# The row numbers of a block's store: from VectorE to GpSimd, and a ring of six

## The reference

```
x = x + tanh(g_xattn[0]) * xattn0(layernorm(x), ctx)      # 16 heads, 120 context rows per batch
x = x + tanh(g_ffn[0])   * ffn0(layernorm(x))             # 8 experts, top 2, silu(x Wg) * (x Wu), then Wd; hidden 688
x = x + tanh(g_xattn[1]) * xattn1(layernorm(x), ctx)
x = x + tanh(g_ffn[1])   * ffn1(layernorm(x))             # 8 experts, top 2, relu(x W1)^2, then W2; hidden 256
```

## Time and profile before

| | |
|---|---|
| median of 3 runs | 711.34 us (710.27 to 711.49) |
| span of the profiled execution | 741.8 us |
| PE busy | 659.3 us (89%) |
| DVE busy | 407.1 us (55%) |
| ACT busy | 271.6 us (37%) |
| POOL busy | 221.4 us (30%) |

### The profile page before, as it was taken

How to read it: one execution, slowest core, us unless ns; L and a number is a source line. 1 busy time by engine, 2 the same in 40 slices (tenths; PEclk the granted TensorE clock), 3 DMA queues, 4 the chain that set the end, 5 groups by cost and what they waited for, 6 DMA issues and landing times.

```text
span 741.8 us, 17801 instructions
## 1 busy us (share of the span) xinstructions
PE 659.3 (89%) x6008; PEld 481.6 (65%) x6008; DVE 407.1 (55%) x1375; ACT 271.6 (37%) x531; POOL 221.4 (30%) x405
## 2 busy tenths in 40 slices
PE   8889887789999999999999999989888888789960
PEld 6657666557777777777775555667666656578730
DVE  3888778774444323332332223688888775554416
ACT  4555555542211111121111112467666432244430
POOL 5123434433231111111111111124655344544430
PEclk9999999999999999999999999999999999899995
DMA  9243434552124111101311100601111132443329
GB/s 231 68 136 124 142 123 169 183 178 67 44 101 120 38 36 29 36 30 36 82 33 41 30 15 18 232 30 31 59 60 59 59 101 86 144 122 115 108 72 339
DMA packets 49960, 69.14 MB, mean 93 GB/s; under 512 B 7751, under 2 KB 37319, under 8 KB 49875
## 3 DMA queue, kind: packets, MB, share of 16 engines
q1 hardware_dynamic: 40620, 49.00, 21.8%
q0 software_dynamic: 6528, 17.90, 6.8%
q10 hardware_dynamic: 2727, 1.11, 0.6%
HBM read 45.76 MB, written 22.23 MB: 92 GB/s over the span
## 4 chain that ended last, share of the span: by engine, by line
PE 70%; DVE 14%; issue 5%; another core or an unknown queue 5%; DMA 2%; ACT 2%; POOL 1%; SPq 0%; ACTq 0%; DVEq 0%; POOLq 0%
PE ps L1764 26%; PE ps L1810 16%; DVE m_rows L981 4%; PE ps L1550 4%; PE ps L1787 3%; PE ps L1488 3%; PE ps L1542 3%; PE ps L1505 2%; PE ps L1588 2%; PE ps L1564 2%; DVE x_sb L965 2%; DVE ctx_q L998 1%; PE ps L1516 1%; DVE share L1003 1%
## 5 line engine op out<-in xcount | busy, mean ns | idle before, releaser
L1764 PE MATMUL ps<-w_all,share 128*128 (+1 forms) x720 | 213.2, 443 | 8.2 <-DVE share L1125 5.8
L1764 PEld LDWEIGHTS ps<-w_all,share 128*128 128x128 f32 (+1 forms) x720 | 125.2, 180 | 73.6 <-issue 13.9
L629 POOL DMA_INDIRECT ys_dram<-share,dest_i x72 | 69.1, 960 | 297.1 <-DVE share L1346 247.5
L1810 PE MATMUL ps<-w_all,share 112*128 (+3 forms) x576 | 139.1, 385 | 5.0 <-ACT share L864 4.3
L1810 PEld LDWEIGHTS ps<-w_all,share 112*128 112x128 f32 (+3 forms) x576 | 98.2, 180 | 24.8 <-issue 8.6
L1405 DVE TENSOR_TENSOR share<-share,ps 128x344 f32<-128x344 f32 x72 | 37.0, 514 | 122.1 <-PE ps L1764 54.1
L981 DVE TENSOR_REDUCE m_rows<-ps 128x8 f32<-128x960 f32 x64 | 70.6, 1143 | 14.4 <-PE ps L1505 9.9
L845 ACT COPY share<-ps 128x512 f32<-128x512 f32 x36 | 21.1, 585 | 141.2 <-PE ps L1787 141.2
L600 POOL DMA_INDIRECT xs_dram<-xn,slot_now x64 | 63.6, 994 | 30.0 <-issue 14.0
L840 ACT ACTIVATE share<-ps 128x344 f32<-128x344 f32 x72 | 32.9, 457 | 96.8 <-PE ps L1764 71.4
L577 POOL TENSOR_SCALAR nm<-mv 128x1 f32<-128x1 f32 (+1 forms) x48 | 11.6, 242 | 157.5 <-DVE mv L1021 120.4
(11 more groups left out here) (235 smaller groups left out, 1102.8 us busy)
## 6 DMA issues: line engine op xcount, KB each, us to landing
w_all<-ys_dram SPq DMA_DIRECT2D x16, 512.0 KB, 7.3
share<-xs_dram SPq DMA_DIRECT2D x56, 129.0 KB
w_all<-gate SPq DMA_DIRECT2D x8, 688.0 KB
w_all<-up SPq DMA_DIRECT2D x8, 688.0 KB
w_all<-down SPq DMA_DIRECT2D x8, 560.0 KB
w_all<-w SPq DMA_DIRECT2D x16, 256.0 KB
share<-xs_dram SPq DMA_DIRECT2D x32, 64.5 KB
out<-x_sb SPq DMA_DIRECT2D x8, 256.0 KB, 5.6
```

The costliest lines, as they stand in the source:

```text
L629: g.indirect_dma_start(ys_dram, bass.IndirectOffsetOnAxis(ap=dest_i[:, u:u + 1], axis=0), y_sb[:, u, :], None).then_inc(D_y[u], 16)
L1764: i = t.matmul(ps[0:r, bank, 0:w], xgT[:, k, 0:r], w_all[:, bass.ds(off + (k * UPW[l] + col - EW[l]), w)], start=(k == 0), stop=(k == KT - 1))
L1810: i = t.matmul(ps[0:n, 6, 0:D], h[:, 0:n], w_all[0:r, bass.ds(off + (KT * UPW[l] + c * D - EW[l]), D)], start=(c == 0), stop=(c == KD[l] - 1))
```

## The change

GpSimd computes the row numbers itself, in `store_block`, just ahead of the DMA that uses them; VectorE's `block_rows` is gone with all its calls. The instruction is a tensor_scalar with `spare` as a scalar per partition, where it was a tensor_tensor. GpSimd now has the waits for `xid` and for the store of three blocks before (`D_y`), and one for its own result. `xid` is a ring of six columns in place of three, so that `x_evac(j)` waits for the row numbers of the block six before, made by GpSimd, and no more for those of the block three before. In layer 0 `y_evac` on VectorE still needs the `D_y` wait for `y_sb`, and now has it behind the wait for TensorE. ScalarE's `y_evac` of layer 1 is as it was.

```diff
-        xid = sb("xid", [P, U3])
+        xid = sb("xid", [P, 2 * U3])
...
             def store_block(l, j):
-                u = j % U3
-                g.wait_ge(d_dest, J0[l] + j + 1)
-                g.wait_ge(e_y, J0[l] + j + 1)
+                J, u, w = J0[l] + j, j % U3, (J0[l] + j) % (2 * U3)
+                g.wait_ge(d_xid, J + 1)
+                need(g, D_y[u], 16 * uses(l, j))
+                g.tensor_scalar(dest_i[:, u:u + 1], xid[:, w:w + 1], spare[:, j:j + 1], None, ALU.min).then_inc(g_dest, 1)
+                g.wait_ge(g_dest, J + 1)
+                g.wait_ge(e_y, J + 1)
                 g.indirect_dma_start(ys_dram, bass.IndirectOffsetOnAxis(ap=dest_i[:, u:u + 1], axis=0),
...
                 def x_evac(j):
...
-                    need(v, d_dest, J - U3 + 1)
-                    v.scalar_tensor_tensor(out=xid[:, u:u + 1], in0=xg[:, u, D + 1:D + 2], scalar=be[:, j:j + 1],
+                    need(v, g_dest, J - 2 * U3 + 1)
+                    v.scalar_tensor_tensor(out=xid[:, w:w + 1], in0=xg[:, u, D + 1:D + 2], scalar=be[:, j:j + 1],
...
-                def block_rows(j):
-                    J, u = J0[l] + j, j % U3
-                    v.wait_ge(d_xid, J + 1)
-                    need(v, D_y[u], 16 * uses(l, j))
-                    v.tensor_tensor(dest_i[:, u:u + 1], xid[:, u:u + 1], spare[:, j:j + 1], ALU.min).then_inc(d_dest, 1)
-
                 def y_evac(j):
-                    block_rows(j)
                     v.wait_ge(b_y, j + 1)
+                    need(v, D_y[j % U3], 16 * uses(0, j))
...
                 def blk1(j, u, first, last):
-                    if j >= 2:
-                        block_rows(j - 2)
...
-                    if last:
-                        block_rows(j - 1)
-                        block_rows(j)
```

More of the change, by code:

```diff
@@ L303, in flamingo_kernel @@
         d_xid = sem("block_tokens_read")
-        d_dest = sem("block_rows_ready")
+        g_dest = sem("block_rows_ready")
         block = es.enter_context(nc.Block())
```

## The result

| | median, us | range | runs |
|---|---|---|---|
| before | 711.13 | 710.02 to 712.81 | 13 |
| after | 713.02 | 711.73 to 717.05 | 13 |

The ratio is 1.003, with an interval of [1.002, 1.004]: some 1.9 us slower. That is just over what the prediction called the least that can be told from no change. The forecast was 710.8, a gain of 0.5.

What follows compares the result with a forecast made beforehand. PE was taken as the whole bound in layer 0's experts and layer 1's steady blocks, with room only at layer 1's start. Terms 0 + 0 - 0.4 - 0.5 + 0.4 + 0 = -0.5 us gave 710.8, range 708.6 to 713.3.

Steps and rivals of the forecast that it cites:

- GpSimd's part at the start of layer 1: +0.4 us: Start of layer 1's experts: added steps for stores 0 to 5 delay GpSimd's list; +0.4 us (-1.35 to +3.1).
- The upper bound of 0.51: Start of layer 1: most that one store was said to cost extra in GpSimd's queue, 0.51 us.
- the deadline's 1.35: Start of layer 1: the store wait moves from VectorE to ScalarE, which needs the landing 1.35 us later.
- Layer 0: 0: Layer 0's experts: removed and added instructions are hidden behind a fully busy PE; 0 us.
- Steady layer 1: 0: Layer 1's steady blocks: VectorE idles for PE and GpSimd has 1.2 us free per block; 0 us.
- The end: 0: Last store: the new instruction and its step fit into 0.79 us of idle; 0 us.
- VectorE's part at the start of layer 1, -0.4: Start of layer 1: VectorE's row numbers leave the path ahead of `x_evac` in two turns; -0.4 us (0 to -0.5).
- its waits for stores, -0.5: Layer 1's steady part: VectorE no longer waits for a late store of three blocks before; -0.5 us (-1.05 to 0).
- The inference on the stops: Waits for "another core or an unknown queue", some 34 us, were suspected to belong largely to the profiled execution.
- GpSimd's list is the bound: Rival, start of layer 1: back-to-back scatters and stores each gain a step; +0.9 to +2.7 us, 713.3, chance 0.19.
- The relief is real: Rival, layer 1: GpSimd has room and VectorE's later deadline is won; -2.8 us, 708.5, chance 0.26.
- A locked port: Rival, start of layer 1: VectorE's square is held until GpSimd's instruction ends; at most 2.4 us, 712.0, chance 0.05.

Runs made afterwards that it cites:

- e16: The changed kernel itself, run again in a set where the kernel before takes 711 us; ratio to before 1.0011.
- e6: The kernel before with only the ring of six for `xid`, VectorE still making the row numbers; ratio to before 0.9999.
- e7: The kernel before with the ring of six and, in layer 1, VectorE's row numbers and their store wait moved behind `x_evac` and the square; ratio to before 0.9991.
- e13: Ring of six, GpSimd making the row numbers in layer 0 only and VectorE in layer 1, in a 711 us set; ratio to before 0.9993.
- e14_crowd_third: Ring of six, GpSimd making the row numbers only for blocks 0 to 13 of layer 1, VectorE all others, 711 us set; ratio to before 1.0036.
- e11: The kernel before with `xid`'s ring of six plus rings of six for `y_sb` and `dest_i` in layer 1, 744 us set; ratio to before 0.9988.
- e18: VectorE making the row numbers, with rings of six for `xid` and, in layer 1, `y_sb` and `dest_i`, in another 744 us set; ratio to before 0.9995.
- e1_before_again: The kernel before, unchanged, profiled a second time; 745.59 us, with a span of 743.9.
- e4: Ring of six, GpSimd making the row numbers only for blocks 0 to 13 of layer 1, VectorE all others, 744 us set; ratio to before 0.9962.
- e10: Repeat, in a 744 us set, of GpSimd making the row numbers only for blocks 0 to 13 of layer 1, VectorE all others; ratio to before 0.9958.
- e12: The changed kernel with rings of six for `y_sb` and `dest_i` in layer 1, 744 us set; ratio to before 0.9948.
- e3: Ring of six, GpSimd making the row numbers in layer 0 and from block 14 of layer 1, VectorE for blocks 0 to 13, 744 us set; ratio 0.9974.
- e17: The changed kernel with layer 1's row numbers of blocks 0 to 2 made earlier, in GpSimd's idle time ahead of the scatters, 744 us set; ratio to before 0.9982.
- e2: Ring of six, GpSimd making the row numbers in layer 0 only and VectorE in layer 1, 744 us set; ratio to before 0.9991.
- e9: Repeat, in a 744 us set, of GpSimd making the row numbers in layer 0 only and VectorE in layer 1; ratio to before 1.0001.
- e5: The changed kernel with one unused column more in `xid`, so that `dest_i` lies elsewhere in memory, 711 us set; ratio to before 1.0032.
- e15: The changed kernel with rings of six for `y_sb` and `dest_i` in layer 1, 711 us set; ratio to before 1.0058.

## Why the prediction was wrong

**The step that failed** is "GpSimd's part at the start of layer 1: +0.4 us", both in its price for one store and in what was set against it.
- *The price.* "A store in a full queue costs 0.24 + 0.28 - 0.30 = 0.22 us more." Measured, a store takes 0.298 + 0.28 + 1.045 + 0.05 = 1.67 us of the list where it took 1.26: 0.41 more. Of the 0.19 that were missing, 0.06 is the instruction (0.30, not 0.24), 0.085 the DMA itself, which grew, and 0.05 the gap ahead of the instruction. The upper bound of 0.51 did hold it. Six stores are 2.5 us; the list grew by 2.7. Alone this is the smaller part of the miss: put into the prediction's own scheme it gives 6 x 0.41 less the deadline's 1.35, that is +1.1 in place of +0.4, and a sum of +0.2 where +1.9 was measured.
- *What was set against it.* The step took 1.3 us of delay and let it cancel against VectorE's deadline, 1.35 us later. No relief is seen in the sum: up to block 12 after and `e16` are 1.0 to 1.6 us slower than the kernels with VectorE's row numbers, not equal to them. The reason that the profiles offer lies in the other ways to PE: the last scatters of the list and the loads behind them have no part in that deadline, and there after lost 1.5 us of PE's time in one wait, 0.7 to 1.5 more than `e6`, `e7` and `e13`. No run takes this way alone away, so its share of the 1.9 is not shown. The prediction named them ("behind GpSimd's new waits stand the last scatters") and gave them no term.

**Terms that held.** Layer 0: 0 (0.9993 in `e13`, PE full). Steady layer 1: 0 (period 2.17, PE 36.00 of 36.00, and 26.1 to 26.2 us for blocks 12 to 24 against 26.0 to 26.1). The end: 0; the last store of after starts 1.13 us behind the last y copy, as in `e6_ring_six` (686.12 against 684.99).

**Terms that can't be seen.** VectorE's part at the start of layer 1, -0.4, and its waits for stores, -0.5: `e7_rows_late` takes both from the path ahead of `x_evac` and has 0.9991 [0.9977, 1.0005], -0.6 us with an interval that holds both 0 and the -0.9 of the two. Of `e6_ring_six`'s seven waits for stores (7.8 us in all) five, 4.2 us, stand in the steady part, where PE is busy 36.00 of 36.00 all the same. The other two are at the start of layer 1, and behind the longer one, 2.78 us, PE waited 1.84 us for VectorE. And `e14_crowd_third`, with VectorE's row numbers in the steady blocks, has one of 2.17 us after which a block took 3.16 us and not 2.17:

```profile
646.68 0.16 DVE L1349 TENSOR_TENSOR dest_i<-xid,spare 128x1 int32<-128x1 f32 x1 [2.17 <-DMA ys_dram<-share,dest_i]
```

So such a wait costs nothing up to some length and then does; in `e6` and `e13` waits of 1.8 and 1.9 us cost 0.05. In the 744-sets, from which the term was read, the steady blocks are 0.3 to 1.1 us shorter with GpSimd's row numbers (26.00 to 26.21 against 26.53 to 27.13). For the most part that isn't this wait: `e11` and `e18`, whose VectorE has no wait for stores there, take 26.57 and 26.60.

**The inference on the stops** was false. They come back in `e1_before_again` and in no profile of a 711-set. What it was used for held up, though: the prediction said that without stops GpSimd's list could be what is late, and it was.

**The rivals.** "GpSimd's list is the bound" is what happened, at the place named (start of layer 1) and under its condition: in after there is no idle time but its own steps between stores 3 and 6. Of ScalarE and VectorE only ScalarE still waits for stores there (6.2 us in four waits). Its term was 6 x 0.22 to 6 x 0.51, less 0.4; with 0.41 it is 2.1, and 1.9 was measured. That the two agree so well is partly luck, since PE loses less in that stage than the list grew, and the -0.4 isn't seen. It had a chance of 0.19. What should have raised it is in the prediction's own sum: nine DMAs back to back against PE's 2.165 us. "The relief is real" needed GpSimd to have room and fell with it in the 711-sets. In the 744-sets it is near to what happened, 0.4 to 0.5% faster in `e4`, `e10` and `e12`. The cause is open. That each added step leaves a gap between DMAs that follow one another at 0.30 us, and that the stops of the other engines then end sooner, fits the steady blocks of `e3`, `e12` and `e17`. It doesn't explain `e4` and `e10`: their lists are 20.4 us long, but so are those of `e2` and `e9` (20.7) with VectorE's row numbers, which gained nothing (0.9991 and 1.0001). "A locked port" fell as a cost: the square L1431 has a median of 416 ns in after and 414 in `e6_ring_six` (there L1436), and only one of 36 takes over 0.5 us, where it meets no row-number instruction. But the two do meet, six times in after from 600 us on, and then it is GpSimd that is held:

```profile
678.86 0.41 DVE L1431 TENSOR_TENSOR share<-share 128x256 f32<-128x256 f32 x1
678.89 0.53 POOL L629 TENSOR_SCALAR dest_i<-xid,spare 128x1 int32<-128x1 f32 x1
```

Started 0.03 us behind a square, the instruction took 0.53 us in place of 0.30, and 0.36 when it started 0.20 behind (641.98); both times it ended 0.15 us after the square. The square stays at 0.41 to 0.42 us in all six. By the rule of the Trainium skill (page "SBUF — State Buffer", section "Who interferes with whom") the two contend, and the one that issues second is blocked; for GpSimd behind a square the trace agrees. For the other order it doesn't show it: a square that started 0.15 us into the instruction (643.86) was no longer than the others. The rival had it the other way round, with VectorE held, and none of the six meetings falls into the list.

## What to carry to other kernels

Before work is moved to an engine "with room", write out that engine's list in the stretch where it has none, instruction by instruction, and follow each end of it (the slot, the ring, the load behind a scatter) to the engine that is the bound; a relief on one of these ways doesn't pay for a delay on another. Price a new instruction ahead of an indirect DMA with all four parts: the gap ahead, itself, the step, and what it does to the DMA. And a profile with waits for "another core or an unknown queue" in a program of one core may show the set of runs and not the kernel: take from it only the terms that don't rest on them. Before two profiles are compared, or a loss of some tenths of a per cent is explained, look at the granted clock stretch by stretch: one fall cost 1.6 to 2.9 us here, as much as the change.

## What the runs showed of the hardware

- An indirect DMA on GpSimd takes 0.96 us on the engine when another engine wrote its row numbers, or GpSimd did so some instructions earlier, and 1.045 when GpSimd's own instruction directly ahead wrote them (in `e17_hoisted` both, in one kernel). By the Trainium skill, page "Perfetto Trace Analysis", section "DMA Instruction — SWDGE (GPSIMD)", such a row ends when the descriptors are written and not when the data has moved; the trace agrees: the last scatter's row in after is 0.97 us long and its landing comes 2.44 us after its start.
- One kernel takes 711 us in some sets and 744 in others. In the slower ones ScalarE and VectorE stand for over 6 us on a semaphore (6.2 in before, 6.5 in `e11`); in the earlier trace rows GpSimd issues indirect DMAs 0.30 us apart meanwhile. The profiles of 711-sets have no such stop.
- In 598 to 603 us PE's granted clock is 1.00 in some profiles of the same work (`e5`, `e6`, `e16`) and 0.50 to 0.57 in others (after, `e7`, `e13`), both with the change and without it; the y copy of block 0 then starts at 600.9 to 601.2 or at 602.6 to 602.8 us. A comparison of two profiles in that stretch has to take pairs with the same clock. In `e15` it was 0.50 in 630 to 635 us, after PE had stood 2.73 us waiting for a load.
- A GpSimd tensor_scalar of one column that starts 0.03 or 0.20 us behind a VectorE tensor_tensor with both inputs in SBUF takes 0.53 or 0.36 us in place of 0.30; the tensor_tensor keeps its 0.41.
